# Two expert-factor tables loaded in one transfer each in place of two halves each, in a two-layer adapted feed-forward kernel

## The reference

```python
hidden_i = einsum('bsd,fd->bsf', x, wi)                       # 128 -> 512
hidden_i += 2 * common_low_rank(x) + 2 * expert_low_rank(x, expert_ids)
hidden_i = relu(hidden_i)
hidden_o = einsum('bsf,df->bsd', hidden_i, wo)                # 512 -> 128
hidden_o += 2 * common_low_rank(hidden_i) + 2 * expert_low_rank(hidden_i, expert_ids)
```

## Time and profile before

| | |
|---|---|
| median of three runs | 481.57 us (480.96 to 481.77) |
| the profiled execution's own time | 480.82 us |
| span of that execution, first to last instruction | 479.0 us |
| PE busy | 474.5 us, 99% of the span |
| PEld, DVE, ACT busy | 395.0, 388.0, 393.6 us |
| POOL busy | 121.7 us, 25% |
| data moved | 27.03 MB, mean 56 GB/s |

### The profile page before, as it was taken

How to read it: one execution, slowest core, us unless ns; L and a number is a source line. 1 busy time by engine, 2 the same in 40 slices (tenths; PEclk the granted TensorE clock), 3 DMA queues, 4 the chain that set the end, 5 groups by cost and what they waited for, 6 DMA issues and landing times.

```text
span 479.0 us, 7437 instructions
## 1 busy us (share of the span) xinstructions
PE 474.5 (99%) x2260; PEld 395.0 (82%) x2260; DVE 388.0 (81%) x638; ACT 393.6 (82%) x543; POOL 121.7 (25%) x102
## 2 busy tenths in 40 slices
PE   9999999999999999999999999999999999999997
PEld 8998888888888888888888888888888888888886
DVE  5898999999989898988889898889897758654343
ACT  4889888888889898888888798898888888697643
POOL 4995212121211212122212121171313144500000
PEclk9999999999999999999999999999999999999999
DMA  8603702021120202020202112120202000000001
GB/s 236 191 24 134 285 0 91 2 88 42 48 88 0 88 0 88 0 88 0 88 1 88 45 43 88 44 90 0 88 2 88 2 0 0 1 1 0 0 23 69
DMA packets 8299, 27.03 MB, mean 56 GB/s; under 512 B 2258, under 2 KB 3602, under 8 KB 6098
## 3 DMA queue, kind: packets, MB, share of 16 engines
q1 hardware_dynamic: 7090, 22.45, 13.4%
q0 software_dynamic: 288, 2.88, 1.7%
q10 hardware_dynamic: 896, 1.38, 1.0%
HBM read 25.26 MB, written 1.44 MB: 56 GB/s over the span
## 4 chain that ended last, share of the span: by engine, by line
PE 96%; POOL 2%; DMA 1%; DVE 0%; SPq 0%; issue 0%; ACT 0%; DVEq 0%
PE bank L538 34%; PE bank L541 34%; PE bank L544 26%; POOL ffn_lo L442 1%; PE bank L638 1%; PE bank L639 1%; DMA stage<-lora_all 1%; PE bank L565 0%; PE bank L562 0%; POOL xlo L447 0%; DVE stage L1076 0%; DVE prod L1076 0%; ACT ffn_hi L842 0%; DVE x L1312 0%; SPq L251 0%
## 5 line engine op out<-in xcount | busy, mean ns | idle before, releaser
L859 ACT ACTIVATE act_out<-bank,vec 128x512 f32<-128x512 f32 x256 | 164.9, 681 | 40.5 <-PE bank L544 28.7
L1154 DVE TENSOR_TENSOR hid_lo<-act_out,hid_hi 128x1024 fp32r<-128x1024 f32 x128 | 158.5, 1258 | 31.6 <-ACT hid_hi L864 31.5
L864 ACT ACTIVATE hid_hi<-act_out 128x1024 fp32r<-128x1024 f32 x128 | 135.9, 1062 | 8.3 <-ACT act_out L859 0.4
L502 POOL TENSOR_TENSOR cur<-cur,prod 128x512 f32<-128x512 f32 x48 | 64.8, 1350 | 233.5 <-DVE prod L1165 233.1
L538 PE MATMUL bank<-hid_hi,moe_hi 128*128 128x512 f32 x256 | 99.8, 390 | 0.0
L544 PE MATMUL bank<-hid_hi,moe_lo 128*128 128x512 f32 x256 | 99.7, 390 | 0.0
L541 PE MATMUL bank<-hid_lo,moe_hi 128*128 128x512 f32 x256 | 99.7, 389 | 0.0
L538 PE MATMUL bank<-xhi,moe_hi 128*128 128x512 f32 x256 | 99.6, 389 | 0.0
L541 PE MATMUL bank<-xlo,moe_hi 128*128 128x512 f32 x256 | 99.6, 389 | 0.0
L544 PE MATMUL bank<-xhi,moe_lo 128*128 128x512 f32 x256 | 99.6, 389 | 0.0
L538 PEld LDWEIGHTS bank<-hid_hi,moe_hi 128*128 128x128 f32 x256 | 48.1, 188 | 11.1
(11 more groups left out here) (134 smaller groups left out, 570.6 us busy)
## 6 DMA issues: line engine op xcount, KB each, us to landing
cw_all<-cw_dram SPq DMA_DIRECT2D x16, 1024.0 KB, 4.7
stage<-ffn_w POOLq DMA_DIRECT2D x1, 2304.0 KB, 8.5
cw_all<-moe_w SPq DMA_DIRECT2D x4, 512.0 KB, 7.5
stage<-lora_all SPq DMA_DIRECT2D x5, 160.0 KB, 4.6
x<-x_t SPq DMA_DIRECT2D x3, 256.0 KB, 5.2
out_t<-x SPq DMA_DIRECT2D x3, 256.0 KB, 2.4
cur<-cond_base ACTq DMA_DIRECT2D x2, 256.0 KB, 3.4
stage<-ffn_w POOLq DMA_DIRECT2D x1, 512.0 KB, 3.9
```

The source lines that it names most:

```text
L502: pool.tensor_tensor(cur[:, c, :], cur[:, c, :], prod[:, s % 2, :], ALU.add).then_inc(add_done, 1)
L859: act.activation(act_out[:, f // 2, f % 2, :], bank[:, f, :], ACT.Gelu_apprx_tanh, bias=vec[:, V_B1 + e * FC + f:V_B1 + e * FC + f + 1]).t ...
L864: act.activation(hid_hi[:, s % 2, 2 * pr:2 * pr + 2, :], act_out[:, pr, :, :], ACT.Copy)\
L1154: dve.tensor_tensor(hid_lo[:, s % 2, 2 * pr:2 * pr + 2, :], act_out[:, pr, :, :], hid_hi[:, s % 2, 2 * pr:2 * pr + 2, :].bitcast(F32), ALU ...
```

## The change

Batches 0 and 1 are loaded with the same `lora_load` as all others: one transfer of 64 rows, 160 KB, in place of two of 32 rows, 80 KB. The separate semaphores for the out factors, `first_out_in`, go. PE therefore waits, ahead of group 0, for all four kinds at once (both semaphores `lora_in[0]` and `lora_in[1]`), and ahead of group 1 for the same semaphores, which are then already up.

```diff
-        first_out_in = [sem(f"first_out_in{b}") for b in range(2)]
...
-        def first_load(queue, b):
-
-            e = lora_expert(queue, b)
-            for kind, arrived in enumerate((lora_in[b], first_out_in[b])):
-                queue.dma_start(lora[lora_rows(b, kind), 0, :],
-                                lora_all[bass.ds(e, 1), 2 * RANK * kind:2 * RANK * (kind + 1), :]
-                                .rearrange("e r n -> (e r) n")).then_inc(arrived, 16)
...
-            first_load(sp, 0)
+            lora_load(sp, 0)
...
-                    pe.wait_ge(first_out_in[b] if j == 1 else lora_in[b], 16)
+                    pe.wait_ge(lora_in[b], 16)
...
-            first_load(act, 1)
+            lora_load(act, 1)
```

## The result

| | before | changed |
|---|---|---|
| median of 14 runs | 481.09 us (480.59 to 482.16) | 481.76 us (481.12 to 482.96) |
| mean of the same runs | 481.22 us | 481.98 us |
| ratio | | 1.0016, 95% interval 1.0009 to 1.0023 |
| the profiled execution's own time | 480.82 us | 482.96 us |
| its span | 479.0 us | 481.2 us |

The changed kernel is slower by 0.8 us (0.4 to 1.1). The forecast time, 481.9 us, is close to the measured 481.76, but that is partly luck: the three runs shown of before had a median of 481.57, the 14 have 481.09. The step itself was forecast as 0.35 us and came out as 0.67 us between the medians and 0.76 us between the means, so two errors cancel in the total.

The account below looks back on a forecast made before the run. PE, busy 99% of the span, was taken as the bound. The first product's delay of 0.35 us, all other terms 0, was added to the median of 481.57, giving 481.9 us; range 480.9 to 482.9.

Parts of the forecast that it names:

- the place and the sign: At the start, PE's first factor product waits longer and the delay goes through whole to the span: slower, +0.07%.
- the prediction's own signs: Wrong if POOL's delay differs from span growth, products behind the pause slow, or the span moves more than the first product.
- the term s: Delay of PE's first factor product ahead of group 0, waiting for whole 160 KB transfers: +0.35 us, landing at 6.05.
- The upper bound of 1.1: Ceiling in us on the first factor product's delay, if SP's first 160 KB takes 4.0 us like its next.
- group 1 delay: Group 1, no longer held back behind group 0, was claimed to cost group 0 nothing: 0 us.
- I add s to the median: The first product's delay, 0.35 us, added to the median of the runs shown, 481.57: 481.9 us.
- The clock rival: Tensor clock falls back in PE's longer pause before the first factor product, losing some 2.2 us: 483.8 us; chance 0.03.
- a pause as short as 0.75 us would change nothing: PE's idle time before the first factor product, 0.75 us in place of 0.4, leaves the clock unaffected.
- I book 0 us: Later transfers issued about 0.3 us earlier on SP and ACT gain nothing; DVE's 0.3 us base-weight wait is off the chain.

Follow-up runs that it names:

- e6: Kernel before with only ACT's transfer for batch 1 made whole, SP's left in halves: 0.11 us over by the median, ratio 1.0007.
- e10: Changed kernel with the base weights of kind 1 issued ahead of batch 3's factors: 0.79 us over the kernel before by the median, ratio 1.0025.
- e5: Kernel before, four transfers of 80 KB kept, but PE waits for all four ahead of group 0: 0.64 us over by the median, ratio 1.0008.
- e3: Kernel before with 9 warm-up products in place of 10, transfers untouched: 0.49 us over by the median, ratio 1.0008.
- e1: The changed kernel itself, timed again: 1.07 us over the kernel before by the median, ratio 1.0019.
- e11: Kernel before with only SP's transfer whole and base weights issued ahead of batch 3's factors: 1.23 us over by the median, ratio 1.0026.
- e2: Changed kernel with 12 warm-up products in place of 10: 0.53 us over the kernel before by the median, ratio 1.0016.
- e7: Kernel before with only SP's transfer for batch 0 made whole: 1.29 us over by the median of five runs, ratio 1.0034.
- e8: Changed kernel with 11 warm-up products: 1.80 us over the kernel before by the median of six runs, ratio 1.0043.
- e4: Kernel before with 11 warm-up products in place of 10: 0.10 us over by the median, ratio 1.0002.
- e12: Kernel before, base weights placed behind ACT's first high part of `x` but issued at practically the same time: 0.07 us over, ratio 1.0005.

## Why the prediction was right, and where it was too small

**Right: the place and the sign.** The bound is PE, and what the start loses the rest of the span hands on: in the changed profile group 4 at +2.1 us, the span at +2.2. In all 14 profiles the execution's time less the start of group 4 is 468.1 to 468.7 us. e6 (first product +0.21, group 4 +0.18) and e10 (+0.71 and +0.71) hand on the first product's delay as forecast.

**Not so in the profile taken: that the first product alone moves the start.** By the prediction's own signs it fails there: the span moves by 2.2 us and the first product by 0.40, POOL starts at 9.77 in place of 8.43, and the products behind the pause take longer (2.08 in place of 1.16 us for the eight of warm-up).

**Right: the term s.** Forecast 0.35, taken from the second half's landing at 6.0. Measured 0.40 and 0.36 (first product at 6.15 and 6.11), with 6.30 to 6.46 where more warm-ups or another order stood ahead. The upper bound of 1.1, from the next 160 KB on SP, was far too high. No group 1 delay was seen: with the clock up, the warm-up products follow 7.31 - 6.11 = 1.2 us behind the first product, before it was 7.18 - 5.75 = 1.4.

**Mis-sized: "I add s to the median".** The sum held this one term, and the change costs 0.8 to 0.9 us by the ratios. What failed is that every other wait stood at nothing. e5, which has only the later start and the longer pause, costs 0.4 to 0.6. Of that, s is about 0.35, by the forecast's working. e3, with the pause alone, costs 0.4 by itself, in the form of executions that are 1 to 1.5 us late. The two don't add up simply, as a late clock hides the other waits.

**The clock rival was given 0.03 and happens.** I priced it at 2.2 us. Of the +2.1 us at group 4 in the changed profile 0.4 is s, so it cost 1.7 there, and 1.5 in e3's. My reason against it was that the pause of 0.4 us "doesn't stop the rise", read from one execution in which it didn't. The rows before showed only that one execution. The profiles show that the time of the rise differs: late in the changed kernel's first profile, early in its second (e1). e3's profile speaks against my reading that a pause as short as 0.75 us would change nothing. PEld waits 0.69 to 1.06 us for the first factors in six profiles; two of them, the change and e3 (0.75 and 0.77 us), have the late rise, and four (e1, e6, e10, e11) haven't, among them the longest pause, e10's. None of the six profiles with 0.23 to 0.47 us has it. That a longer pause makes the late rise more frequent is what e3's times suggest (6 of 12 at 481.96 or more, against 2 of 35). A rival that happens in some of the executions should have stood in the sum with its share, not only among the chances.

**"I book 0 us" for the earlier queues** was right in its effect and wrong in its reason. I held that DVE's 0.3 us for the base weights was off the chain. It is off it by little: in e5's and e1's profiles it is the chain. And the earlier issue brought no earlier landing: issued at 4.23 in place of about 4.6, they landed at 9.5 in place of 8.6.

**What stays open.** SP's whole transfer (e2, e7, e8, e10, e11, and the change) comes out 0.8 to 2.1 us over by the ratios, ACT's alone 0.3; the later start explains 0.4 to 0.6 of it. The remainder goes with late landings of the transfers behind it in several profiles, but these are late in e3's and e4's too, where the first transfers are untouched. The base weights landed at 8.6, 9.2, 9.9 and 9.0 us in the four profiles with the transfers and order of before (before, e3, e4, e12), and at 9.5, 10.8, 10.4 and 9.5 in the four of the changed kernel (the change, e1, e2, e8), though they were issued 0.4 us sooner there. This points to the whole transfers making them late, but the two ranges overlap and eight profiles don't settle it. Nor is e8's median explained.

No version tried here beats the kernel before.

## What to carry to other kernels

Joining two transfers makes the first use wait for the last byte: look at who needs the first half first, and price the join by when the second half lands now. Here the shortened issue queue was worth nothing: the transfers issued earlier landed later, with the 16 transfer engines at a busy share of 0.93 or more from 6.1 to 14.7 us in the changed profile. Where a start-up is hung between several transfers and a clock that still has to rise, one profile is one draw: compare the spread and the groups of the times before a term is called hidden, and put a rival that strikes in some executions into the sum with its share.

## What was not expected of the hardware

- With two queues issuing 256 KB each within 0.3 us, the one issued first landed first, by 0.6 to 1.2 us: 9.1 and 10.3 us in e7 (SP first, 4.38 and 4.60), 9.5 and 10.1 in the changed kernel (ACT first, 4.23 and 4.38).
- In the four profiles of the changed kernel, whose transfers are the same, the 256 KB of base weights took 5.3, 6.6, 6.2 and 5.3 us from issue to landing (the change, e1, e2, e8).
- A pause of 2.08 us of PE, at the upper clock level, was followed, after about 0.9 us of work at that level, by 3.4 us at the lower (e11). The six slowest runs of the case all have the mean clock of such a fall, 0.996.
